# Attention in groups of four query tiles, with the context kept in columns

## The reference

```python
q, k, v = x @ Wq + bq, x @ Wk + bk, x @ Wv + bv      # 16 heads of 32 features
scores = einsum('bhqd,bhkd->bhqk', q / sqrt(32), k) + attention_bias
scores = where(src_mask, -inf, scores)               # one row of flags per batch
probs  = softmax(scores, axis=-1)
ctx    = einsum('bhqk,bhkd->bhqd', probs, v)         # back to (B, S, 512)
x      = x + (ctx @ Wo + bo)
h      = layernorm(x) * g2 + beta2
return x + gelu2(h @ W1 + b1) @ W2 + b2
```

## Time and profile before

| | us |
|---|---|
| three runs | 3473.83, 3475.27, 3478.54 |
| median | 3475.27 |
| the profiled execution | 3475.8, its span 3474.0 |
| embed stage | 0 to 490 |
| attention | 490 to 2492 |
| feed-forward | 2492 to 3474 |

### The profile page before, as it was taken

How to read it: one execution, slowest core, us unless ns; L and a number is a source line. 1 busy time by engine, 2 the same in 40 slices (tenths; PEclk the granted TensorE clock), 3 DMA queues, 4 the chain that set the end, 5 groups by cost and what they waited for, 6 DMA issues and landing times. The chain is left out here.

```text
span 3474.0 us, 84659 instructions
## 1 busy us (share of the span) xinstructions
PE 3408.8 (98%) x33299; PEld 2692.7 (78%) x33299; DVE 2343.6 (67%) x5039; ACT 2278.9 (66%) x3399; POOL 2395.8 (69%) x942
## 2 busy tenths in 40 slices
PE   7999989999999999999999999999999999999998
PEld 3444448888888888888888888888778888887886
DVE  7776758888888888888888888888623232332333
ACT  2433449999999999999999999999622212221321
POOL 1222249999999999999999999999643324232322
PEclk8999999999999999999999999999999999999998
DMA  6666599888898988898888998888644544564463
GB/s 215 225 235 239 197 367 349 325 337 331 333 401 329 338 331 333 341 389 337 332 332 329 367 370 334 331 327 329 246 144 154 167 137 157 164 191 143 154 210 124
DMA packets 342721, 954.80 MB, mean 275 GB/s; under 512 B 33204, under 2 KB 190004, under 8 KB 267576
## 3 DMA queue, kind: packets, MB, share of 16 engines
q1 hardware_dynamic: 337108, 940.95, 73.4%
q10 hardware_dynamic: 5220, 8.42, 0.6%
HBM read 849.63 MB, written 99.62 MB: 273 GB/s over the span
## 5 line engine op out<-in xcount | busy, mean ns | idle before, releaser
L1249 POOL TENSOR_TENSOR at_tiles<-at_tiles,at_negmask 128x1920 f32<-128x1920 f32 x509 | 1950.7, 3896 | 29.9 <-DMA at_tiles<-in_bias 19.0
L1349 ACT ACTIVATE at_tiles<-at_tiles,at_rmin 128x2048 f32<-128x2048 f32 x512 | 1030.5, 2013 | 2.4 <-DVE at_rmin L1409 2.4
L1288 PE MATMUL at_ps_p<-consts,at_tiles 128*128 128x128 f32 x8192 | 1023.6, 272 | 1.7 <-ACT at_prob_t L1359 1.3
L1288 PEld LDWEIGHTS at_ps_p<-consts,at_tiles 128*128 128x128 f32 x8192 | 936.3, 139 | 72.5 <-DVE at_prob_t L1420 2.0
L1359 ACT ACTIVATE at_prob_t<-at_ps_p 128x512 f32<-128x512 f32 x1664 | 898.2, 603 | 125.0 <-PE at_ps_p L1288 124.9
L1409 DVE CUSTOM_DVE_ANT_0 at_tiles<-at_ps_s,at_tiles,at_rmin 128x1024 f32<-128x1024 f32 x512 | 655.0, 1279 | 171.7 <-PE at_ps_s L1273 171.0
L1267 PE MATMUL at_ps_s<-at_k_stack,at_q_stack 128*128 128x512 f32 x2048 | 700.7, 438 | 8.1 <-DVE at_rmin L1409 6.1
L1409 DVE CUSTOM_DVE_ANT_0 at_tiles<-at_ps_s,at_tiles 128x1024 f32<-128x1024 f32 x512 | 623.9, 1219 | 24.5 <-POOL at_tiles L1249 22.2
L1307 PE MATMUL at_ps_c<-at_prob_t,at_v 128*32 128x128 f32 x16384 | 500.3, 274 | 1.0 <-DVE at_ctx_rows L1437 1.0
L1307 PEld LDWEIGHTS at_ps_c<-at_prob_t,at_v 128*32 128x32 f32 x16384 | 431.6, 110 | 44.2 <-issue 43.0
L1267 PEld LDWEIGHTS at_ps_s<-at_k_stack,at_q_stack 128*128 128x128 f32 x2048 | 310.8, 191 | 62.5 <-issue 51.5
(11 more groups left out here) (239 smaller groups left out, 4098.3 us busy)
## 6 DMA issues: line engine op xcount, KB each, us to landing
at_tiles<-in_bias SPq DMA_DIRECT2D x512, 1024.0 KB, 6.3
ff_w_card<-w_mix SPq DMA_DIRECT2D x256, 256.0 KB, 2.7
ff_w_card<-in_W SPq DMA_DIRECT2D x192, 256.0 KB, 2.9
at_k_stack<-k_hi SPq DMA_DIRECT2D x128, 256.0 KB, 5.6
at_k_stack<-k_lo SPq DMA_DIRECT2D x128, 256.0 KB, 5.6
negm<-em_mask_out SPq DMA_DIRECT2D x32, 512.0 KB, 6.5
at_q_stack<-q_hi SPq DMA_DIRECT2D x128, 128.0 KB, 5.3
at_q_stack<-q_lo SPq DMA_DIRECT2D x128, 128.0 KB, 5.3
```

The lines of the kernel that those rows point to most:

```text
L1249: pool.tensor_tensor(tiles[s][:, 0:PCOLS], tiles[s][:, 0:PCOLS], negm[s][:, 0:PCOLS], ALU.add).then_inc(s_pool, 1)
L1288: last = pe.transpose(ps_p[k][:, y * P:(y + 1) * P], tiles[s][:, t * P:(t + 1) * P], ident)
L1349: act.activation(tiles[s][:, :], tiles[s][:, :], ACT.Exp, bias=rmin[:, s, 1:2], scale=-1.0, accum_out=rsum[:, s:s + 1]).then_inc(s_exp, 1)
```

## The change

Attention works in groups of four units.

- `pv` runs once per group. Each of the four units has one group of 32 array columns over all 16 key tiles, so the sum is whole and the context of the four stands in 128 partitions as columns: 32 features x 128 queries per unit. The number of V instructions per unit is unchanged.
- The copied probabilities are in five buffers of one unit (`NPT`) in place of two of two units.
- The reciprocals: DVE takes them with each row sum repeated over 32 columns (128x128 in one instruction, `invert`), PE transposes that (`rinv_columns`), DVE copies the result to SBUF (`take_rinv`) and multiplies the context with it (`context`). `parts`, `parts_rows` and the two-part sum are gone: per group one transpose where there were two, and three DVE operations where there were ten.
- SP stores the 64 KB of a group two units into the next (`store`), where ACT stored a whole half batch after its last head. The scratch tensor in HBM holds blocks of 128x128 in columns.
- The mask is added by POOL in 1856 columns and by PE in 192.
- The orders of PE, ACT and DVE are written anew. On PE, V of the group before now stands after the second chunk of transposes of the first unit.
- In the feed-forward stage the context is loaded as columns, in 16 loads of 64 KB per tile (`read_ctx`), and goes to the product with Wo as it is. `ctx_columns` and `take_ctx` are gone. The first two banks of that product may change places (`row_bank`), and with them the waits ahead of it.

The diff, cut to its core (the lines that it removes stand in the functions above):

```diff
-    at.pool_columns = S - 128
+    at.pool_columns = S - 192
...
-    at.p_t = [sb(f"at_prob_t{i}", [P, 2, S // P, P]) for i in range(2)]
+    at.p_t = [sb(f"at_prob_t{i}", [P, S // P, P]) for i in range(4)]
...
-    at.cx_sb = sb("at_ctx_parts", [P, P])
-    at.cx_all = sb("at_ctx_rows", [P, RING, D])
+    at.p_t += [sb("at_prob_t4", [P, S // P, P])]
+    at.cx_t = [sb(f"at_ctx_t{i}", [P, P]) for i in range(2)]
+    at.rinv_t = sb("at_rinv_t", [P, P])
...
-    at.rinv = sb("at_rinv", [P, 2])
+    at.rinv = sb("at_rinv", [P, 4, HD])
...
-    NP = NU // 2
+    NG = NU // 4
...
+    NPT = 5
...
                 _, _, b, qh, h = place(n * RING)
-                after(sp, s_pv, 4 * (n - 1))
+                after(sp, s_pv, 2 * (n - 1))
...
-                sp.dma_start(net.cx[:], net.ctx.rearrange("(t j p) d -> t p j d", j=TJ, p=P)[0]).then_inc(net.s_cx, 16)
+                sp.wait_ge(s_st[0], 16 * HEADS)
+                net.read_ctx(sp, 0)
...
+            def store(g):
+                if not 0 <= g < NG:
+                    return
+                n, s, b, qh, h = place(4 * g)
+                sp.wait_ge(s_cxo, g + 1)
+                sp.dma_start(net.ctx[(b * QH + qh) * 2 + s // 4, h], cx_t[g % 2][:]).then_inc(s_st[g % 2], 16)
...
                             load_kq(n + 1)
                         if s == 2:
                             load_v(n + 1)
+                        if s % 4 == 2:
+                            store(2 * n + s // 4 - 1)
             load_ffn()
+            for g in range(NG - 3, NG):
+                store(g)
+            for i in range(2):
+                sp.wait_ge(s_st[i], 16 * NG // 2)
...
-            def pv(pr):
-                if not 0 <= pr < NP:
+            def pv(g):
+                if not 0 <= g < NG:
...
-                n = pr * 2 // RING
-                after(pe, s_cxo, 2 * pr)
-                if pr % 4 == 0:
+                n = 4 * g // RING
+                pe.wait_ge(s_rc, g + 1)
+                if g % 2 == 0:
                     pe.wait_ge(s_vin[n % 2], 16 * (n // 2 + 1))
-                for u in (2 * pr, 2 * pr + 1):
+                for u in range(4 * g, 4 * g + 4):
                     for c in range(CH):
                         k, i = bank(u, c)
                         pe.wait_ge(s_pe[k], i + 1)
-                for i in range(QUART):
-                    for g in range(4):
-                        half, j = divmod(g, 2)
-                        t = half * QUART + i
-                        last = pe.matmul(ps_c[g * HD:(g + 1) * HD, 0:P], v_sb[n % 2][:, t, :], p_t[pr % 2][:, j, t, :],
-                                         start=(i == 0), stop=(i == QUART - 1))
+                for t in range(KT):
+                    for j in range(4):
+                        last = pe.matmul(ps_c[j * HD:(j + 1) * HD, 0:P], v_sb[n % 2][:, t, :], p_t[(4 * g + j) % NPT][:, t, :],
+                                         start=(t == 0), stop=(t == KT - 1))
                 last.then_inc(s_pv, 1)
 
-            def parts_rows(pr):
-                if not 0 <= pr < NP:
+            def rinv_columns(g):
+                if not 0 <= g < NG:
                     return
-                pe.wait_ge(s_cxs, pr + 1)
-                pe.transpose(ps_c[:, P:2 * P], cx_sb[:], ident).then_inc(s_cxm, 1)
...
+                pe.wait_ge(s_rv, g + 1)
+                after(pe, s_cxo, g)
+                pe.transpose(ps_c[:, P:2 * P], rinv[:].rearrange("p j d -> p (j d)"), ident).then_inc(s_rt, 1)
+
+            for g in range(-3, NG + 2):
+                u = 4 * g
                 qk(u + 4, 0)
+                transposes(u, (1,))
+                pv(g - 1)
+                transposes(u, (2,))
+                qk(u + 4, 1)
+                transposes(u, (3,))
+                qk(u + 5, 0)
                 transposes(u + 1, (0, 1, 2))
-                pv(pr - 1)
-                qk(u + 4, 1)
-                qk(u + 5, 0)
+                qk(u + 5, 1)
                 transposes(u + 1, (3,))
-                transposes(u + 2, (0, 1))
-                qk(u + 5, 1)
-                parts_rows(pr - 1)
-                transposes(u + 2, (2, 3))
+                transposes(u + 2, (0,))
                 qk(u + 6, 0)
+                transposes(u + 2, (1, 2))
+                qk(u + 6, 1)
+                transposes(u + 2, (3,))
+                qk(u + 7, 0)
                 transposes(u + 3, (0, 1, 2))
-                pv(pr)
-                qk(u + 6, 1)
-                qk(u + 7, 0)
+                rinv_columns(g)
                 transposes(u + 3, (3,))
-
+                qk(u + 7, 1)
+                transposes(u + 4, (0,))
...
-                after(act, s_pv, pr - 1)
+                after(act, s_pv, (u - NPT) // 4 + 1)
                 act.wait_ge(s_pt[k], i + 1)
-                act.activation(p_t[pr % 2][:, j, 4 * c:4 * c + 4, :].rearrange("p t q -> p (t q)"), ps_p[k][:],
+                act.activation(p_t[u % NPT][:, 4 * c:4 * c + 4, :].rearrange("p t q -> p (t q)"), ps_p[k][:],
                                ACT.Copy).then_inc(s_pe[k], 1)
...
+            for g in range(-3, NG + 2):
+                u = 4 * g
+                exp(u - 3)
+                take(u - 4, 1)
+                take(u - 4, 2)
+                take(u - 4, 3)
+                take(u - 3, 0)
+                take(u - 3, 1)
+                take(u - 3, 2)
+                take(u - 3, 3)
+                take(u - 2, 0)
+                exp(u)
                 take(u - 2, 3)
-                exp(u)
+                take(u - 1, 0)
                 take(u - 1, 1)
-                exp(u + 1)
+                take(u - 1, 2)
                 take(u - 1, 3)
...
                 exp(u + 2)
-                take(u + 1, 1)
...
-                if not 0 <= pr < NP:
+                s = 4 * g % RING
+                dve.wait_ge(s_exp, 4 * g + 4)
+                after(dve, s_rt, g)
+                v.reciprocal(rinv[:], rsum[:, s:s + 4].unsqueeze(2).broadcast_to([P, 4, HD])).then_inc(s_rv, 1)
...
+            def take_rinv(g):
+                if not 0 <= g < NG:
                     return
-                dve.wait_ge(s_pv, pr + 1)
...
+                dve.wait_ge(s_rt, g + 1)
+                v.tensor_copy(rinv_t[:], ps_c[:, P:2 * P]).then_inc(s_rc, 1)
...
+            def context(g):
+                if not 0 <= g < NG:
+                    return
+                dve.wait_ge(s_pv, g + 1)
+                dve.wait_ge(s_rc, g + 1)
+                after(dve, s_st[g % 2], 16 * (g // 2))
+                v.tensor_tensor(cx_t[g % 2][:], ps_c[:, 0:P], rinv_t[:], ALU.mult).then_inc(s_cxo, 1)
+
+            for g in range(-3, NG + 2):
+                u = 4 * g
                 scores(u + 6, 0)
-                take(u + 3, 2)
-                take(u + 3, 0)
+                take(u + 2, 1)
+                take(u + 2, 2)
                 scores(u + 6, 1)
-                parts(pr)
                 scores(u + 7, 0)
+                take_rinv(g)
+                scores(u + 7, 1)
+                scores(u + 8, 0)
+                take(u + 4, 0)
+                invert(g + 1)
+                scores(u + 8, 1)
+                scores(u + 9, 0)
+                context(g)
+                scores(u + 9, 1)
...
+        def row_bank(n, j):
+
+            return (j + chain_bank(n - 1, 1)) % 2 if j < 2 else j
...
             def load_cx(n):
-                sp.wait_ge(s_ct, 4 * n)
-                sp.dma_start(cx[:], cxv[n]).then_inc(s_cx, 16)
+                sp.wait_ge(s_wo, 4 * n)
+                net.read_ctx(sp, n)
...
                 for c in range(DC):
-                    pe.wait_ge(s_ct_out, 4 * (n - 1) + c + 1)
+                    if n >= 3:
+                        pe.wait_ge(s_xt_out, 4 * (n - 3) + c + 1)
                     to_columns(hn, c, s_ht)
 
             def out_project(n):
                 p = n - 1
+                pe.wait_ge(s_cx, 4 * DC * 16 * (n + 1))
                 for j in range(TJ):
-                    if n >= 2 and j == chain_bank(p, 0):
-                        pe.wait_ge(s_f_out, n - 1)
                     if n >= 1:
-                        if j < 2:
-                            pe.wait_ge(s_taken, taken(p, "g21", 0 if j == chain_bank(p, 0) else 1))
+                        if j == 0:
+                            pe.wait_ge(s_taken, taken(p, "g21", 1))
+                        elif j == 1:
+                            pe.wait_ge(s_taken, taken(p, "g21", 0))
+                            after(pe, s_f_out, n - 1)
                         elif j == 2:
                             pe.wait_ge(s_sum, added(p, "c12", 1))
                         else:
                             pe.wait_ge(s_sum, added(p, "c11", 1))
                     for k in range(DC):
-                        pe.wait_ge(s_ct_out, 4 * n + k + 1)
-                        last = pe.matmul(ps_m[j][:], t2[:, k, j * P:(j + 1) * P], wo[:, k, :],
```

(50 more changed lines are left out.)

84 lines of the change are left out of this document (8 added, 76 removed).

## The result

The changed kernel takes 3588.1 us (3580.2 to 3594.9 in four runs) against 3475.0: the ratio is 1.032 (1.030 to 1.035). It is 113 us slower; the forecast was 3500 with a range of 3392 to 3535. The profiled execution took 3586.8 us, span 3585.0.

What follows compares the result with a forecast made beforehand. TensorE was taken to pace attention, POOL 1.2% behind; after the change a late bias reload would set each head. 3475.8 + 31 (reload) + 9 (mask changes) - 16 (feed-forward) = 3500 us, range 3392 to 3535.

Steps and rivals of the forecast that it cites:

- TensorE's own time: Attention, matrix engine: a group of four units takes 14.93 us against 15.51; alone, 74 us would go.
- the axis: Forecast start times of TensorE's steps inside one group, from unit 4's first scores at 0 to the next group at 14.93.
- a run of 64 V instructions 1.89, and 64 more cost 16 x .11 = 1.74, so 3.63: Price of the joined V run in a group on TensorE: 128 instructions take 3.63 us.
- The reload: Bias tiles in attention: the second unit's bias queues behind key and query loads, 1.8 us late per head; +31 us taken.
- unit 11: Place without slack in the next group: its masked tile is wanted at 28.6 us and ready at 30.4.
- Rival A: Attention: the reload keeps up and TensorE's 14.93 us per group stands, total 3393 us; chance .24.
- Rival B: DVE's reciprocal ahead of scores 4b: eight cycles per column, 1.1 us for 128, a group 15.5 to 15.6; chance .08.
- Rival C: Attention's bias reload is worse: bursts make the landing 8.5 us or more, total over 3535 us; chance .09.
- The changes of the mask: Three places in attention where negative masks go through the same queue and POOL's lead is gone: 3 x 3 = +9 us.
- The mask: Masked halves of scores on TensorE: 64 more mask columns add about .03 us, .64 in place of .61.
- The feed-forward stage: After attention: the context's 16 transposes per tile go, 12.6 us plus 3.5 in the first tile, together -16 us.

Runs made afterwards that it cites:

- a_ks_vfar: Kernel with spread key loads (3542), with V's run in two halves far apart, the second some 4 us after the first: 3595.4 us.
- a_ks_vfar2: Spread key loads and V in two halves far apart, with DVE's first-chunk copy moved ahead and reciprocals transposed and copied one step earlier: 3451.6 us, ratio .993.
- a_kspread: Changed kernel (3588) with the eight key and query loads in four pairs, behind the bias of the fifth to eighth unit, for the pass after next: 3542.1 us.

## Why the prediction was wrong

- **TensorE's own time** was right at its best: 14.92 us measured as the sum of the least steps, 14.93 forecast. The medians add to 15.3, the axis is too short mostly at 5a to 5b (up to 1.9 for 1.78, the reciprocal) and 7a to 7b (2.47 for 2.32). The step that failed is "a run of 64 V instructions 1.89, and 64 more cost 16 x .11 = 1.74, so 3.63". From the first V instruction to the transposes behind, a run of 128 takes 3.63 us at the median, but 4.06 on average. In the trace of the changed kernel 23 runs hold a stall of .6 to 3.0 us (from one start to the next), 47 us together. Each ended 1.2 to 1.6 us after the end of a 16 KB packet of queue q8, and they lie about 618, 868 or a sum of these matmuls apart. Both speak for TensorE having used up its instructions and waited for the next block. That is argued from the times of the packets and not shown: no run changed the supply itself. That halves far apart have no stalls, at the same number of instructions, is shown by a_ks_vfar and a_ks_vfar2. With the "issue" waits outside V (19 us) the stalls come to 1.0 per pass, and the clock stood at .50 for 27 us of attention (530 to 2480 us; in the kernel before, never), half of it lost, .2 per pass.
- **The reload** was right as a mechanism, not in size. Forecast: landing 7.3 us after issue, POOL waiting 3 to 4 us for the second unit, 1.8 late per pass. Measured: 7.2 at the median, waits of 3.95, 2.89 and 1.59 in a row, 2.8 on average. What TensorE lost ahead of the first scores of units 4 and 7 was 1.4 per pass over the least, most of it at the pass's first scores, where it waited for the keys, and only .3 at unit 11, which the prediction had named. It needed V ahead of the tile's last transposes, as the prediction had it: without that the same burst costs some 4 us or less.
- **The keys** were missing. In the trace the bias of the first unit was issued at 1207.5 and TensorE was released by the last key load at 1217.1, 9.6 us later; it wanted them after 8.5 (14.93 - 6.4). It cost nothing beside the bias (3591 against 3588), but by the sum's own logic it should have been a term.
- So a pass: 29.84 for the least of each step, 1.4 ahead of the scores that waited for the reload and the keys, 1.1 in the steps with V, .7 spread over the others, together 33.0; forecast 31.5. 63 x 1.5 = 95, and 88 us were missed. The parts don't simply add: with the reload mended (46 us net of the 80) the stalls grew (51.6 to 70.9 us), so one partly covered the other. Why they grew is not shown.
- **Rival A** has its condition, a reload that keeps up, in a_kspread, but its 3393 was reached by no run: a group came near 14.93 only in the best passes (30.0 us in the changed kernel), and the best kernel here is at 3442. **Rival B**: the reciprocal takes .95 us, near the eight-fold estimate of 1.1, not .3, and at its place it cost some .1 us per group. (953 - 163)/126 = 6.3 ns per column, against 1.1 for a column of scores. The Trainium skill (VectorE: DVE Perf Modes, the walkthrough of the 8-slice pipeline) says that it is iterative with a repeat count of 8, and the trace agrees in kind; an estimate by that count would be 8.8. **Rival C**'s number came true, by another mechanism than its longer landing.
- **The changes of the mask**: 9 us forecast; the three passes behind them took 2.4, 1.6 and 2.6 us over the median pass, 6.6 together.
- **The mask**: .03 us per unit forecast on TensorE; .01 measured in the order before, .02 where all masks stand ahead of transposes. **The feed-forward stage**: 16 forecast, 13.4 measured. Its first product took 15.5 us until the transposes behind it where the kernel before took 14.4, so the first tile gave less; why is not shown.
- The range ended at 3535, since the price of TensorE was given no upper bound: three bounds were drawn around the landing, none around the run of V, though no row of the kernel before showed a run of more than 64.

## What to carry to other kernels

A price taken from one start to the next holds for the stretch in which it was seen; where a change joins two dense stretches of short instructions into one, bound its price from above, and look for waits called "issue". Before shortening the engine that sets the pace, list for each buffer when it is freed, what its refill queues behind and when its next user wants it, keys as well as tiles. Where no engine is full after a change, move single instructions apart: here another order of instructions and loads, with the mask's constant set back, was worth 146 us.

## What the hardware showed that was not expected

- A stall of TensorE can cost more than itself: after some of 1.9 to 3.3 us the granted clock went to .50 and stood there for 3.4 us, after one of 3.0 us it did not. From 530 to 2480 us that came to 27 us in the changed kernel, 48 with the spread keys, and none in the kernel before or with the halves of V far apart.
- Dense stretches of V's instructions stalled at 128, and at 64 + 64 with four transposes between, not at 96 or at 64 + 64 far apart; each of the 23 stalls in V's runs of the changed kernel ended 1.2 to 1.6 us behind a packet of the instruction queue.
- A DVE copy of 128 columns within SBUF took .23 to 3.84 us, 123 of 128 ending .07 to .10 behind one of POOL's instructions; the reciprocal, also within SBUF, took .944 to .955 in all 128 cases.
